# First six loads of gated values asked for one by one ahead of the down pass, with its first stores and code loads taken phase by phase

## The chip, the core and the metric

The kernel runs on one core of one Trainium2 chip. The metric is the device time of one execution in microseconds (us), as the median of several runs. Five engines work side by side, each in its own program order, and wait for one another by semaphores: TensorE (PE, matmuls, with a row PEld for weight loads), VectorE (DVE), ScalarE (ACT), GpSimd (POOL) and SyncE (SP). In this kernel POOL and SP mostly ask for DMA transfers, which the core's 16 DMA engines carry out.

## What is computed

Cross attention over a context, added to x, and then a feed-forward network whose three weight matrices are stored as 4-bit codes with one scale for each block of 64. The feed-forward part is what matters here:

```python
def dequant_nf4(q, absmax, shape):
    w = NF4_CODE[q.reshape(-1)]
    w = w.reshape(-1, BLOCK) * absmax[:, None]
    return w.reshape(shape)
Wg = dequant_nf4(gate_q, gate_absmax, (M, HD))
Wu = dequant_nf4(up_q, up_absmax, (M, HD))
Wd = dequant_nf4(down_q, down_absmax, (HD, M))
g = jnp.einsum('bsh,mh->bsm', x, Wg)
u = jnp.einsum('bsh,mh->bsm', x, Wu)
h = jax.nn.silu(g) * u
return jnp.einsum('bsm,hm->bsh', h, Wd)
```

HD is 1024, M is 3584, x has 8 x 256 rows. The codes come as 32-bit integers.

## The kernel before

**Stages.** Attention first, then the gate and up product, then the down product. Both products use a scheme of seven block products where a plain one has eight (Strassen's kind), and every operand is split into a high and a low float16 half (three matmuls for one product).

**Gate and up.** PE works through 392 slots (SLOT_COUNT) of 12 matmuls of 128 x 512. A slot reads a weight piece from one of the nine places of the tile wS. DVE and ACT combine and empty the PSUM banks, and form the gated values h (silu(g) times u). They are made for 14 pairs of chunks (CH_PAIRS), in seven forms and two sides for each pair. ACT copies a form's high half into one of four buffers, hst (line 2298), DVE writes its low half (line 2362), and POOL stores the buffer to the HBM tensor keep_h (line 2156). A buffer is free for the next copy when its store has landed.

**Down.** PE works through 98 steps (DOWN_STEPS, index m): seven groups (one for each form), of 14 steps each (one for each pair). Step m needs 512 KB of gated values, which POOL loads back from keep_h into one of six places, m % 6 (H_RING; line 2167): four in the tile `tail`, two in wS. It needs a decoded and transposed down weight too. A step is 24 matmuls, three in each of the eight banks. At the end of a group DVE empties the banks (lines 2404, 2410 and 2419), behind whatever DVE has in front of it, and PE's next group waits bank by bank. At step 0 each bank waits until DVE has taken the last gate and up results from it (line 2331); the third bank waits for all of them.

**Decode.** A unit is 128 x 512 codes. POOL or SP loads it into one of three places of the tile q (256 KB; line 285 for gate and up, line 288 for down). ACT makes ten squares (lines 343 and 347), DVE multiplies the factors (lines 376 and 363), both split the result into halves (lines 415, 422 and 431), and SP transposes it by DMA (line 302). There are 56 down units; their code loads begin during the last slots. The load of unit u waits until ACT has finished unit u − 3 and DVE has begun it. A planner (PLAN) lays down at which phase (slot or down step) each decode operation and each load stands in its engine's program order. Nothing else ties the engines' progress together but the semaphores.

**POOL's order.** In each slot k: the stores that are due (`stores_due`), the code loads that are due (`loads_due`) and, in the last four slots, one load of gated values (`load_h`). Then a wait until PE has ended all slots, and loads 4 and 5, whose places lie in wS. Step 0 of the down pass begins with the stores of three phases, then the code loads of three phases, then load 6. POOL carries this out strictly in order: an instruction that can't go on holds all that stand behind it.

Of the kernel before, what the change touches and what calls it, by code (L numbers as in the profile page):

```python
# [60 lines left out]
Q_RING, HALF_RING, SLOTS = 3, 5, 9  # L61
# [22 lines left out]
GATE_UP_PIECES = PIECES * STAGES  # L84
# [78 lines left out]
def piece_done(z):  # L163

    return slot_of(z // PIECES, z % PIECES, 1) + 1
# [1852 lines left out]
def feed_forward(nc, t, un, streams, st):  # L2018
# [6 lines left out]
    EVICT_BANK = {P2: X, P7: V, P3: Z, P4: Y}  # L2025
    EVICT_PLACE = {P2: (0, 0), P7: (1, 1), P3: (0, 1), P4: (1, 0)}
    HST_RING, H_RING = 4, len(t.h_in)
    EARLY_H = 4
    Q_AHEAD, ROWS_AT, Y_AT = 3, 1, 3
    BANKS = 8  # L2030
    FORM_BUF = {H_A11: 0, H_A22: 1, H_S1: 1, H_A12: 3, H_S3: 2, H_S2: 0, H_S4: 3}
    SUM_FORMS = (H_S1, H_S3, H_S2, H_S4)
    LAST_IN_BUF = (H_S2, H_S2, H_S3, H_S4)
# [26 lines left out]
    def down_freed(m):  # L2060

        group, c = m // CH_PAIRS, m % CH_PAIRS
        return (s_dn, BANKS * (group + 1)) if c == CH_PAIRS - 1 else (s_hd, (CH_PAIRS - 1) * group + c + 1)

# [81 lines left out]
    def gpsimd(pool):  # L2146
# [11 lines left out]
        def load_h(m):  # L2158
            if m < DOWN_STEPS:
                group, pair = m // CH_PAIRS, m % CH_PAIRS  # L2160
                form = GROUP_FORM[group]
                if m >= H_RING:
                    pool.wait_ge(*down_freed(m - H_RING))
                for side in range(2):
                    n = form_number(pair, form, side)
                    pool.wait_ge(s_hst[n % HST_RING], ring_count(n, HST_RING))
                nc.gpsimd.dma_start(t.h_in[m % H_RING].rearrange("p n a d -> p n (a d)"), t.hs[form, pair]).then_inc(s_hl[m % H_RING], 16)

        for k in range(SLOT_COUNT):
            stores_due(k)  # L2170
            loads_due(HIDDEN_PHASE + k)
            if k >= SLOT_COUNT - EARLY_H:
                load_h(k - SLOT_COUNT + EARLY_H)
        pool.wait_ge(s_mm, SLOT_COUNT)
        for m in range(EARLY_H, H_RING):
            load_h(m)
        for m in range(DOWN_STEPS):
            for ahead in range(Q_AHEAD) if m == 0 else (Q_AHEAD - 1,):
                if m + ahead < CH_PAIRS:
                    stores_due(SLOT_COUNT + m + ahead)  # L2180
            if m == 0:
                for ahead in range(Q_AHEAD):
                    loads_due(DOWN_PHASE + ahead)
            load_h(m + H_RING)
            loads_due(DOWN_PHASE + m + Q_AHEAD)
# [292 lines left out]
```

## Time and profile before

| what | value |
|---|---|
| median of 3 runs | 1928.77 us |
| lowest and highest run | 1926.29 and 1930.59 us |
| the profiled execution: its own time | 1936.15 us |
| the profiled execution: span in the trace | 1934.4 us |
| busy in the span: PE, PEld | 1899.4 us (98%), 961.7 us (50%) |
| busy in the span: DVE, ACT, POOL | 1624.6 us (84%), 1454.3 us (75%), 372.0 us (19%) |
| chain that ended last | PE 65%, ACT 15%, DVE 7%, issue 5%, DMA 2% |

Busy shares are means over stages with different limits. The chain that ended last is followed back from the last instruction: at each step to what released it. A timeline row gives the start, the duration, engine, line, operation, what is written and read, and in square brackets how long the engine had been idle before and on whom it waited. Idle time on an engine that isn't last costs nothing.

### The profile page before, as it was taken

How to read it: one execution, taken by the hardware profiler on the slowest of the kernel's cores; microseconds unless marked ns; L12 is line 12 of the kernel's file. 1: busy time of each engine (PE TensorE's matmuls, PEld its weight loads, DVE VectorE, ACT ScalarE, POOL GpSimd, SP SyncE). 2: the span in 40 equal slices, each digit the busy share in tenths (PEclk: the TensorE clock that was granted, in tenths of full speed). 3: DMA queues.
4: the chain of work that ended last, by engine and by line, in shares of the span. 5: the costliest groups of instructions: out<-in, count | busy, mean ns of one | idle time of the engine just before them, and what ended most of it. 6: DMA issues, size and time to landing. Idle time of an engine off the chain costs nothing.

```text
span 1934.4 us, 29450 instructions
## 1 busy us (share of the span) xinstructions
PE 1899.4 (98%) x9742; PEld 961.7 (50%) x9742; DVE 1624.6 (84%) x2673; ACT 1454.3 (75%) x2704; POOL 372.0 (19%) x570
## 2 busy tenths in 40 slices
PE   8999999999999999999999999999999999999999
PEld 3478888644444444444444444444443444444444
DVE  7968999878898898898898898898788898896963
ACT  2987676577988988988988988988979999900000
POOL 0013344321111121121121121121123222210010
PEclk9999999999999999999999999999999999999999
DMA  9347999954565464565464564555499999874462
GB/s 352 70 82 171 260 260 274 297 177 109 116 152 117 118 162 122 112 156 126 115 158 120 115 158 121 115 152 125 115 191 237 244 224 232 227 252 131 162 229 86
DMA packets 439257, 326.15 MB, mean 169 GB/s; under 512 B 373696, under 2 KB 373696, under 8 KB 437184
## 3 DMA queue, kind: packets, MB, share of 16 engines
q1 hardware_dynamic: 392848, 170.35, 40.8%
q0 software_dynamic: 44032, 153.65, 25.3%
q8 instruction: 77, 1.26, 0.3%
q10 hardware_dynamic: 2224, 0.27, 0.1%
q14 instruction: 76, 0.62, 0.1%
HBM read 154.31 MB, written 82.31 MB: 122 GB/s over the span
## 4 chain that ended last, share of the span: by engine, by line
PE 65%; ACT 15%; DVE 7%; issue 5%; DMA 2%; SPq 1%; POOL 0%; DVEq 0%; ACTq 0%; POOLq 0%
PE ps L2210 39%; PE ps L2252 19%; PE ps L1609 5%; ACT sq L347 5%; ACT sq L343 4%; ACT w L347 1%; PE ps L1577 1%; DVE w L363 1%; ACT w L343 1%; DVE tail L2362 1%; ACT halves L415 1%; PE ps L1644 1%; ACT tail L2283 1%; DMA T<-tail 1%; DVE halves L431 1%
## 5 line engine op out<-in xcount | busy, mean ns | idle before, releaser
L2210 PE MATMUL ps<-T,wS 128*128 128x512 f16 x4704 | 1017.6, 379 | 4.1 <-DVE ps L2317 2.5
L2210 PEld LDWEIGHTS ps<-T,wS 128*128 128x128 f16 x4704 | 459.8, 98 | 558.3 <-issue 4.8
L347 ACT ACTIVATE sq<-sq 128x512 f32<-128x512 f32 x898 | 515.1, 624 | 0.0
L363 DVE SCALAR_TENSOR_TENSOR w<-sq,w 128x512 f32<-128x512 f32 x590 | 416.5, 706 | 114.4 <-ACT sq L347 104.5
L343 ACT ACTIVATE sq<-q 128x512 f32<-128x512 int32 x598 | 361.9, 629 | 55.3 <-DVE w L363 47.7
L2252 PE MATMUL ps<-T,tail 128*128 128x512 f16 x1584 | 347.0, 380 | 10.0 <-DMA tail<-keep_h 3.6
L2252 PEld LDWEIGHTS ps<-T,tail 128*128 128x128 f16 x1584 | 155.0, 98 | 199.6 <-issue 13.7
L431 DVE SCALAR_TENSOR_TENSOR halves<-w,halves 128x512 f16<-128x512 f32 x240 | 163.8, 692 | 6.5 <-ACT halves L415 6.2
L2252 PE MATMUL ps<-T,wS 128*128 128x512 f16 x768 | 168.4, 379 | 0.2 <-DVE tail L2419 0.2
L2156 POOL DMA_DIRECT2D keep_h<-tail x196 | 106.3, 542 | 295.3 <-DVE tail L2362 294.7
L415 ACT CAST halves<-w 128x512 f16<-128x512 f32 x204 | 125.9, 619 | 41.2 <-DVE w L363 31.6
L2362 DVE SCALAR_TENSOR_TENSOR tail<-tail 128x512 f16<-128x512 f32 x196 | 133.7, 682 | 10.4 <-ACT tail L2298 10.2
L1609 PE MATMUL ps<-T 128*128 128x256 f16 x1152 | 128.7, 273 | 0.0
L2298 ACT CAST tail<-tail 128x512 f16<-128x512 f32 x196 | 119.6, 611 | 5.5 <-DVE tail L2331 5.5
L2252 PEld LDWEIGHTS ps<-T,wS 128*128 128x128 f16 x768 | 74.7, 98 | 91.4 <-DVE tail L2419 1.4
L1609 PEld LDWEIGHTS ps<-T 128*128 128x128 f16 x1152 | 112.6, 98 | 13.2 <-DMA T<-tail 0.3
L285 POOL DMA_DIRECT2D q<-in_L_ffn_up_q x52 | 28.0, 538 | 353.0 <-DVE w L363 256.9
L1508 POOL TENSOR_TENSOR T<-tail,T 128x256 f16<-128x256 f32 x64 | 58.9, 921 | 170.1 <-ACT T L1740 170.1
L288 POOL DMA_DIRECT2D q<-in_L_ffn_down_q x56 | 42.5, 759 | 229.5 <-DVE w L363 103.1
L2331 DVE SCALAR_TENSOR_TENSOR tail<-ps,up_out,tail 128x512 f32<-128x512 f32 x112 | 83.5, 746 | 2.1 <-PE ps L2210 1.1
L2283 ACT ACTIVATE tail<-ps,gate_out 128x512 f32<-128x512 f32 x112 | 75.8, 676 | 6.1 <-DVE ps L2321 3.7
L400 DVE TENSOR_TENSOR w<-w 128x512 f32<-128x512 f32 x112 | 76.8, 704 | 1.3
(229 smaller groups left out, 1870.5 us busy)
## 6 DMA issues: line engine op xcount, KB each, us to landing
keep_h<-tail POOLq DMA_DIRECT2D x196, 256.0 KB, 2.6
tail<-keep_h POOLq DMA_DIRECT2D x66, 512.0 KB, 4.9
wS<-keep_h POOLq DMA_DIRECT2D x32, 512.0 KB, 5.3
q<-in_L_ffn_down_q POOLq DMA_DIRECT2D x56, 256.0 KB, 4.4
T<-in_x SPq DMA_DIRECT2D x13, 1024.0 KB, 8.5
q<-in_L_ffn_up_q POOLq DMA_DIRECT2D x52, 256.0 KB, 3.0
q<-in_L_ffn_gate_q POOLq DMA_DIRECT2D x48, 256.0 KB, 3.5
keep_x<-T SPq DMA_DIRECT2D x38, 256.0 KB, 4.9
```

What stands on the lines that cost most here:

```text
L343: nc.scalar.activation(place, un.q[:, ring, :], ACT.Square, bias=b, scale=a).then_inc(un.s_act, 1)
L347: nc.scalar.activation(place, place, ACT.Square, bias=b, scale=a).then_inc(un.s_act, 1)
L363: nc.vector.scalar_tensor_tensor(out=out, in0=square_place(un, u, i - 1), scalar=FACTORS[i - 1][1], in1=un.w[:, buf, :], op0=ALU.add, op1= ...
L415: nc.scalar.copy(un.halves[:, z % HALF_RING, 0, :], source_of(un, t, z)).then_inc(un.s_whi, 1)
L431: nc.vector.scalar_tensor_tensor(out=un.halves[:, z % HALF_RING, 1, :], in0=source_of(un, t, z), scalar=1.0, in1=un.halves[:, z % HALF_RIN ...
L1609: last = nc.tensor.matmul(r_bank(o), t.A[:, a, k, o * P:(o + 1) * P], xT(b)[:, c, k, :], start=k == 0 and j == 0, stop=k == KT - 1 and j = ...
L2156: nc.gpsimd.dma_start(t.hs[form, pair, :, side, :], t.hst[:, n % HST_RING].rearrange("p a d -> p (a d)")).then_inc(s_hst[n % HST_RING], 16)
L2210: last = nc.tensor.matmul(ps[:, bank, :], un.wS[:, z % SLOTS, a, kt, :], t.Tp[side][product][:, :, b, kt, :], start=fresh and n == 0, stop ...
L2252: last = nc.tensor.matmul(ps[:, j, :], h[:, j // PAIRS, a, tok], quad(q, c)[:, b].rearrange("p k d -> p (k d)"), start=fresh and n == 0, s ...
L2283: nc.scalar.activation(t.act_buf[e], ps[:, EVICT_BANK[product] + side, :], ACT.Silu, scale=t.gate_out[:, 2 * pair + row:2 * pair + row + 1 ...
L2298: nc.scalar.copy(t.hst[:, n % HST_RING, 0, :], t.act_buf[2 * FORM_BUF[form] + side]).then_inc(s_hhi, 1)
L2362: nc.vector.scalar_tensor_tensor(out=t.hst[:, n % HST_RING, 1, :], in0=t.act_buf[2 * FORM_BUF[form] + side], scalar=1.0, in1=t.hst[:, n % ...
```

## The change

`EARLY_H` goes. A table H_AT names six slots, 26, 22, 18, 14, 8 and 4 before the end of the gate and up pass, and in each of them POOL now asks for one load of gated values, 0 to 5, behind that slot's stores and code loads. Loads 4 and 5 write into wS, whose pieces PE still reads then. They no longer wait for the end of all slots; each waits until PE has ended the last piece that was put into the places it overwrites (H_IN_W; pieces 190 and 192, ended by slots 382 and 386 in a count from one). At the start of the down pass the first three phases are taken one by one, stores and then code loads, where the stores of all three stood ahead of the code loads of all three.

```diff
-    EARLY_H = 4
+    H_AT = {SLOT_COUNT - at: m for m, at in enumerate((26, 22, 18, 14, 8, 4))}
...
+    H_IN_W = {m: max(z for z in range(GATE_UP_PIECES) if z % SLOTS in (2 * m - 8, 2 * m - 7)) for m in (4, 5)}
...
                 if m >= H_RING:
                     pool.wait_ge(*down_freed(m - H_RING))
+                elif m in H_IN_W:
+                    pool.wait_ge(s_mm, piece_done(H_IN_W[m]))
...
         for k in range(SLOT_COUNT):
             stores_due(k)
             loads_due(HIDDEN_PHASE + k)
-            if k >= SLOT_COUNT - EARLY_H:
-                load_h(k - SLOT_COUNT + EARLY_H)
-        pool.wait_ge(s_mm, SLOT_COUNT)
-        for m in range(EARLY_H, H_RING):
-            load_h(m)
+            if k in H_AT:
+                load_h(H_AT[k])
         for m in range(DOWN_STEPS):
             for ahead in range(Q_AHEAD) if m == 0 else (Q_AHEAD - 1,):
                 if m + ahead < CH_PAIRS:
                     stores_due(SLOT_COUNT + m + ahead)
-            if m == 0:
-                for ahead in range(Q_AHEAD):
+                if m == 0:
                     loads_due(DOWN_PHASE + ahead)
             load_h(m + H_RING)
             loads_due(DOWN_PHASE + m + Q_AHEAD)
```

Only POOL's order changes. On POOL, in the stretch from the last slots to the start of the down pass, stood before (keep_h<-tail is a store of gated values, tail<-keep_h and wS<-keep_h are the loads of them, q<-in_L0_ffn_down_q is a code load):

```order
L2156 DMA keep_h<-tail 128x1024 [waits s_hlo_f]
L288 DMA q<-in_L0_ffn_down_q 128x4x128 [waits s_fac,s_act]
L2167 DMA tail<-keep_h 128x2048 [waits s_hst1_f,s_hst0_f]
L2156 DMA keep_h<-tail 128x1024 [waits s_hlo_f]
L2167 DMA tail<-keep_h 128x2048 [waits s_hst3_f,s_hst2_f]
...
L2167 DMA wS<-keep_h 128x2048 [waits s_hst1_f,s_hst0_f,s_mm]
L2167 DMA wS<-keep_h 128x2048 [waits s_hst3_f,s_hst2_f]
L2156 DMA keep_h<-tail 128x1024 [waits s_hlo_f] x2
L288 DMA q<-in_L0_ffn_down_q 128x4x128 [waits s_fac,s_act] x2
L2167 DMA tail<-keep_h 128x2048 [waits s_hst1_f,s_hst0_f,s_hd_f]
```

and the same stretch, from load 4 on, stands now so:

```order
L288 DMA q<-in_L0_ffn_down_q 128x4x128 [waits s_fac,s_act] x3
L2170 DMA wS<-keep_h 128x2048 [waits s_hst1_f,s_hst0_f,s_mm]
L288 DMA q<-in_L0_ffn_down_q 128x4x128 [waits s_fac,s_act]
L2157 DMA keep_h<-tail 128x1024 [waits s_hlo_f]
L288 DMA q<-in_L0_ffn_down_q 128x4x128 [waits s_fac,s_act]
L2170 DMA wS<-keep_h 128x2048 [waits s_hst3_f,s_hst2_f,s_mm]
L2157 DMA keep_h<-tail 128x1024 [waits s_hlo_f] x4
L288 DMA q<-in_L0_ffn_down_q 128x4x128 [waits s_fac,s_act]
L2157 DMA keep_h<-tail 128x1024 [waits s_hlo_f]
L288 DMA q<-in_L0_ffn_down_q 128x4x128 [waits s_fac,s_act]
L2170 DMA tail<-keep_h 128x2048 [waits s_hst1_f,s_hst0_f,s_hd_f]
```

The six loads, which stood together with four stores, have moved out from between them. The first of the two code loads ahead of load 6 (unit 9) now stands behind four stores and ahead of one, where it stood behind all five.

Also on POOL, at the first down-code load, where the earliest of the six loads now stands; before, none stood here:

```order
L288 DMA q<-in_L0_ffn_down_q 128x4x128 [waits s_fac,s_act]
L2156 DMA keep_h<-tail 128x1024 [waits s_hlo_f] x5
L288 DMA q<-in_L0_ffn_down_q 128x4x128 [waits s_fac,s_act]
L2156 DMA keep_h<-tail 128x1024 [waits s_hlo_f] x4
L288 DMA q<-in_L0_ffn_down_q 128x4x128 [waits s_fac,s_act]
```

and now:

```order
L288 DMA q<-in_L0_ffn_down_q 128x4x128 [waits s_fac,s_act]
L2157 DMA keep_h<-tail 128x1024 [waits s_hlo_f] x2
L2170 DMA tail<-keep_h 128x2048 [waits s_hst1_f,s_hst0_f]
L2157 DMA keep_h<-tail 128x1024 [waits s_hlo_f] x3
L288 DMA q<-in_L0_ffn_down_q 128x4x128 [waits s_fac,s_act]
L2157 DMA keep_h<-tail 128x1024 [waits s_hlo_f]
L2170 DMA tail<-keep_h 128x2048 [waits s_hst3_f,s_hst2_f]
L2157 DMA keep_h<-tail 128x1024 [waits s_hlo_f] x3
```

Loads 0 and 1 stand among stores of gated values, three of which follow each of them directly.

## Rows read from the trace of the kernel before

**Rows 1.** Windows, middle of the down pass: columns in the first line, x counts instructions

```profile
core 0: us, PE busy (x) PEld busy (x) DVE busy (x) ACT busy (x) POOL busy (x), PEclk, DMA share, GB/s
1480.00:1600.00 120.00, 118.25 (x548) 52.93 (x547) 107.01 (x178) 120.00 (x232) 30.92 (x48) 1.00 1.00 236
```

**Rows 2.** Timeline of PE, down pass until the start of group 3

```profile
1412.28 1.46 PE L2252 MATMUL ps<-T,tail 128*128 128x512 f16 x6 [2.09 <-issue]
1414.60 19.60 PE L2252 MATMUL ps<-T,tail 128*128 128x512 f16 x90 [0.86 <-DVE tail L2331]
1434.04 10.52 PE L2252 MATMUL ps<-T,wS 128*128 128x512 f16 x48
1444.40 5.34 PE L2252 MATMUL ps<-T,tail 128*128 128x512 f16 x24
1450.45 5.34 PE L2252 MATMUL ps<-T,tail 128*128 128x512 f16 x24 [0.70 <-DMA tail<-keep_h]
1458.73 12.21 PE L2252 MATMUL ps<-T,tail 128*128 128x512 f16 x48 [2.94 <-DMA tail<-keep_h]
1470.77 10.52 PE L2252 MATMUL ps<-T,wS 128*128 128x512 f16 x48
...
1493.25 10.52 PE L2252 MATMUL ps<-T,tail 128*128 128x512 f16 x48 [1.60 <-DVE tail L2404]
...
1566.09 10.52 PE L2252 MATMUL ps<-T,wS 128*128 128x512 f16 x48 [0.16 <-DVE tail L2419]
...
1640.54 20.88 PE L2252 MATMUL ps<-T,tail 128*128 128x512 f16 x96 [1.78 <-DVE tail L2410]
```

**Rows 3.** Windows, the stretch behind PE's longest wait (columns as in rows 1)

```profile
1460.00:1464.00 4.00, 4.00 (x14) 1.52 (x13) 3.29 (x6) 4.00 (x9) 1.56 (x3) 0.66 1.14 173
```

**Rows 4.** Timeline of ACT around its wait for a code load

```profile
1410.53 2.19 ACT L347 ACTIVATE sq<-sq 128x512 f32<-128x512 f32 x4
...
1428.90 1.15 ACT L347 ACTIVATE w<-w 128x512 f32<-128x512 f32 x2
...
1437.03 1.15 ACT L343 ACTIVATE sq<-q 128x512 f32<-128x512 int32 x2 [6.99 <-DMA q<-in_L_ffn_down_q]
```

**Rows 5.** Timeline of POOL: code loads (L288), a store (L2156), loads (L2167)

```profile
1394.92 0.76 POOL L288 DMA_DIRECT2D q<-in_L_ffn_down_q  x1 [5.44 <-DVE w L363]
...
1413.59 1.13 POOL L2167 DMA_DIRECT2D wS<-keep_h  x2
...
1421.55 0.55 POOL L2156 DMA_DIRECT2D keep_h<-tail  x1 [5.45 <-DVE tail L2362]
1431.08 0.77 POOL L288 DMA_DIRECT2D q<-in_L_ffn_down_q  x1 [8.98 <-DVE w L363]
1437.38 0.76 POOL L288 DMA_DIRECT2D q<-in_L_ffn_down_q  x1 [5.53 <-issue]
...
1442.40 0.55 POOL L2167 DMA_DIRECT2D tail<-keep_h  x1
...
1447.54 0.53 POOL L2167 DMA_DIRECT2D tail<-keep_h  x1 [0.58 <-issue]
```

**Rows 6.** Issue to landing (last number, us): DMAs of 1413.6, 1421.6, 1431.1, 1442.4, 1447.5, 1408.2

```profile
wS<-keep_h POOLq DMA_DIRECT2D x2, 512.0 KB, 17.5
...
keep_h<-tail POOLq DMA_DIRECT2D x1, 256.0 KB, 13.7
...
q<-in_L_ffn_down_q POOLq DMA_DIRECT2D x1, 256.0 KB, 5.9
...
tail<-keep_h POOLq DMA_DIRECT2D x1, 512.0 KB, 7.9
...
tail<-keep_h POOLq DMA_DIRECT2D x1, 512.0 KB, 11.1
...
keep_h<-tail POOLq DMA_DIRECT2D x1, 256.0 KB, 4.7
```

**Rows 7.** Timeline of POOL and ACT: a store, and the copy that reuses its buffer

```profile
1345.18 0.54 POOL L2156 DMA_DIRECT2D keep_h<-tail  x1 [1.85 <-DVE tail L2362]
...
1352.40 0.60 ACT L2298 CAST tail<-tail 128x512 f16<-128x512 f32 x1
```

## The prediction

> **What bounds the kernel now.** I read the busy time of the engines by stretches first, then TensorE (PE) in order of time around the start of the down pass, then the GpSimd queue (POOL), the landing times of its DMAs, and ScalarE (ACT) and VectorE (DVE) beside them. In the down pass PE is nearly full, but it isn't alone: from 1480 to 1600 us PE works 118.25 of 120 us, and ACT, which decodes the down weights, works 120.00 of 120 [rows 1]. So there are two chains that run side by side, PE's steps and the ACT/DVE decode, and they meet where DVE has to empty the PSUM banks between groups.
>
> PE's steps: two steps (48 matmuls) take 1444.40 − 1434.04 = 10.36 us, so a step is 5.18 us and a matmul 0.216 us [rows 2]. What PE loses after 1410 stands in its idle notes [rows 2]: 2.09 us before step 0, 0.86 us at its third bank, which waits for DVE's last eviction; 0.70 us and 2.94 us at steps 7 and 8, for loads of gated values; 1.60, 0.16 and 1.78 us at 1493.25, 1566.09 and 1640.54, the starts of groups 1, 2 and 3, where DVE's eviction is late. Steps 6 to 9 take 1470.77 − 1444.40 = 26.37 us instead of 20.72: a loss of 5.65 us, of which 3.64 is shown as idle time. Much of the rest is the clock: from 1460 to 1464 us the granted clock is 0.66, between its two levels of 2.4 and 1.2 GHz, just after the idle 2.94 us [rows 3].
>
> The decode: ACT ends a unit's squares at 1428.90 + 1.15 = 1430.05 and then idles 6.99 us, until 1437.03, for a code load [rows 4]. That load, unit 9 (the tenth down-code request), is asked for by POOL at 1431.08 and takes 5.9 us to land [rows 5, 6]. Its counters ask only that ACT has finished unit 6 (1410.53 + 2.19 = 1412.72 [rows 4]) and DVE has begun it. POOL's last instruction before it, a store, began at 1421.55 and ended at 1422.10, so POOL stood 9 us with its named conditions fulfilled [rows 5]. What does end then is the landing of the two loads of gated values issued at 1413.59 and right after: 17.5 us, thus about 1431.1 to 1431.7 [rows 5, 6]. The next code load starts at 1437.38, 0.35 us after the one before landed, with no releaser that the profile can name [rows 5]. I read this as a limit on what POOL's DMA queue can hold: six loads of 512 KB put in within 7 us block the next code load, and a code load is blocked until an earlier one is consumed. Six of them are 3 MB, and stores lie among them.
>
> **Part 1: the six loads leave the crowd.** They are the same instructions, each asked for once. POOL time is unchanged; it has idle time before nearly each of them. The first now stands just ahead of the store at 1345.18 [rows 7], the fifth just behind the code load at 1394.92 [rows 5], the sixth two code loads later, where the first stood. The values are of pairs 0 to 5 and were stored long before. Loads 4 and 5 wait for PE's slots 382 and 386, which end 10 and 6 slots ahead of PE's change to the down pass at 1410.2: at 2.59 us a slot, 1384.3 and 1394.6. POOL reaches load 4 only after 1394.92 + 0.76 [rows 5], and load 5 later still. No new wait ends last, cost 0; were POOL early, a code load would stand behind it.
>
> Step 0 now finds its load: the 2.09 us go. But the third bank still waits for DVE's eviction, until 1414.60 [rows 2], and nothing here makes that eviction earlier. So these 2.09 us come back as waiting, 2.95 in place of 0.86 us plus the six matmuls, and the gain is 0.
>
> **Part 2: code loads and stores, phase by phase.** POOL now asks for code load 9 before the store that began at 1421.55, thus between 1413, when unit 6 is finished, and 1422.10. Either is enough: with the 5.9 us of [rows 6] it lands between 1419 and 1428, before 1430.05. So on its own this interleaving is worth 0, and the work that hides it is unit 8 on ACT; it gives code load 10 some room. Code load 10 needs unit 7 finished on ACT. ACT does 232 operations in 120 us [rows 1], 0.517 us each, and a unit has ten: 5.2 us. So unit 7 ends about 1424.9. Asked for then, code load 10 may take 10.3 us before ACT wants it at 1435.2. Load 6 follows at about 1425.6 instead of 1438, loads 7 and 8 at about 1435 and 1440 instead of 1442.40 and 1447.54 [rows 5]. With their old 7.9 and 11.1 us [rows 6] they land at 1443 and 1451; steps 7 and 8 begin without gaps at 1449.6 and 1454.8. The 0.70 and 2.94 us go, and the clock's part with them.
>
> **The sum.** PE alone could win a lot: without a gap from 1414.60, group 3 would start 42 steps less six matmuls later, 217.56 − 1.30 = 216.26, at 1630.86 instead of 1640.54: 9.68 us. But there DVE's eviction ends last, and it stands behind the decode. That chain has no other idle time worth the name between 1437.03 and 1640; so it moves by what it idles now, 6.99 us. Group 1, whose start waits for DVE, goes from 1493.25 to 1486.3 where PE alone gives 1485.8; group 2 at 1559.1 (PE 1558.8), group 3 at 1633.5. After group 3 PE runs through and nothing gives the gain back. The sum is 6.99 us, with 0 and 9.68 us as the ends.
>
> At step 0 there is one unknown, the clock. Now the idle time there is in two pieces; afterwards it is one piece of some 3.1 us, a little over the 2.94 us that was followed by the lower clock [rows 2, 3]. If that happens, PE loses 5.65 − 3.64 = 2.0 us, at most. Group 1 then starts at 1487.8 and group 2 at 1560.3, later than DVE allows; at group 3 DVE ends last again, and the loss is absorbed. From below it costs 0; I take 0 for the end time.
>
> A page of the Trainium skill bears on the landing times. The row says 17.5 us for a load of 512 KB in the crowd [rows 6]. The Trainium skill's "DMA: Bandwidth & Descriptors", section "Anatomy of one DMA — SWDGE (gpsimd) path", fits a DMA's time as 2.0 us plus its bytes over 436 GB/s, 3.2 us by an estimate for 512 KB, and some 12 us for the six and four stores together. By that rule the crowd would be gone when POOL is through its stores at 1422.10, no code load would be held, and the time would be that of the first rival below; the row contradicts it.
>
> **Rivals.**
>
> *The hold stays* (no gain). If POOL stands at 1422 for another reason than landings, the decode chain moves by 0. PE still wins its 5.65 us at steps 6 to 9 and then waits for DVE at 1493.25 as long as now. Time unchanged, 1928.8. For it: the profile names DVE as releaser at 1431.08. Against it: that counter was satisfied long before, and two starts agree with landings to within half a microsecond.
>
> *The load moves but lands slowly* (half the gain). Transposes keep the DMA engines busy in this stretch: a store of 256 KB issued at 1421.55 took 13.7 us [rows 6]. At that price code load 9 lands at 1429.8, just in time, but code load 10 at 1424.9 + 13.7 = 1438.6 instead of 1435.2. The chain gives back 3.4 us and 3.6 remain: 1925.2. Against it: without 3 MB ahead of it that store would hardly take this long.
>
> *The crowd moves to the stores* (slower). From 1343 on, each of the first loads stands ahead of stores, which free the four buffers into which ACT copies gated values. The store of 1345.18 must have landed when ACT copies at 1352.40 [rows 7]: 7.2 us of room. A store behind a load took 4.7 us at 1408 [rows 6]; as slow as in the crowd, 13.7, it would hold ACT 6.5 us at each of two places, loads 0 and 1. That is 13.0 less the 7.0 won: 6.0 us slower, 1934.8. It decides when a store takes over about 7 us. The rule beside it: the Trainium skill's "Trainium Kernel Development and Optimization", section "Key Constraints", says that DMAs issued from the three queues share the same 16 engines and interleave, so an earlier load is not free.
>
> *PE alone decides* (more gain). If DVE weren't the last at groups 1 to 3, up to 9.68 us: 1919.1.
>
> **How the numbers follow.** The profiled execution took 1936.15 us with a span of 1934.4, the runs have a median of 1928.77. The difference lies outside the stretches used, so the 7.0 us are taken from the median: 1921.8; a profiled execution should give about 1929.2. Chances: forecast 0.68, half the gain 0.14, no gain 0.10, slower 0.05, more gain 0.03. The range reaches from the PE bound, 1919.0, over the half gain to 1926.5, with about 1 us for the spread of runs (1926.3 to 1930.6). About 0.2%, 3.9 us, is what a measurement of this kernel can tell from no change: 1924.9 is the line. Nearly all of the forecast's and the larger gain's chance lies below it, and little of the half gain's: faster 0.72, same 0.23, slower 0.05.
>
> **What would show it.** Code load 9 asked for at 1415 to 1423, with no wait of ACT for down codes near 1430. Loads 4 and 5 landing in under 9 us. No PE wait for gated values after step 0, and the start of group 3 about 7 us earlier against the change to the down pass. Step 0's first two banks start at once, and the third still waits for DVE. I am wrong if ACT still idles there, if ACT's copies wait for stores between 1345 and 1365, or if DVE's eviction delays take back what PE won.

## The result, and the profile after

| what | before | after |
|---|---|---|
| median of 17 runs each, side by side | 1927.04 us | 1931.62 us |
| lowest and highest run | 1926.14 and 1933.53 us | 1928.55 and 1938.69 us |
| the profiled execution: its own time | 1936.15 us | 1929.53 us |
| the profiled execution: span | 1934.4 us | 1927.7 us |

The kernel became slightly slower: the ratio after/before is 1.0019, with a 95% interval from 1.0010 to 1.0028, or 3.7 us (1.9 to 5.4); the two medians lie 4.6 us apart. 1921.8 us was forecast, with a range up to 1926.5. The two traced executions say the opposite: after's is 6.6 us the shorter. So the first thing to see is that before's traced execution lies 9.1 us above the median of its own kernel, and after's 2.1 us below.

Timeline of PE in the kernel after, around the start of the down pass and at the start of group 3 (columns as in [rows 2]; the down pass stands at L2251 now):

```profile
1409.62 1.46 PE L2251 MATMUL ps<-T,tail 128*128 128x512 f16 x6
1415.08 21.29 PE L2251 MATMUL ps<-T,tail 128*128 128x512 f16 x90 [3.99 <-DVE tail L2330]
1436.20 10.52 PE L2251 MATMUL ps<-T,wS 128*128 128x512 f16 x48
1446.56 20.88 PE L2251 MATMUL ps<-T,tail 128*128 128x512 f16 x96
1467.28 7.93 PE L2251 MATMUL ps<-T,wS 128*128 128x512 f16 x36
...
1633.91 20.88 PE L2251 MATMUL ps<-T,tail 128*128 128x512 f16 x96 [0.71 <-DVE tail L2409]
```

Against [rows 2], the 2.09 us ahead of step 0 and the 0.70 and 2.94 us of steps 7 and 8 are gone, and groups 1 and 2 start without a gap. The wait at the third bank has grown from 0.86 to 3.99 us. From that bank to the start of group 3 it is 1633.91 − 1415.08 = 218.83 us, before 1640.54 − 1414.60 = 225.94: 7.11 us won, where 6.99 was the forecast.

Timeline of POOL after. The third down-code load with load 2 behind it, then the stretch of [rows 5]:

```profile
1360.50 0.77 POOL L288 DMA_DIRECT2D q<-in_L_ffn_down_q  x1 [3.15 <-DVE w L363]
1361.26 0.54 POOL L2157 DMA_DIRECT2D keep_h<-tail  x1
1361.79 0.54 POOL L2170 DMA_DIRECT2D tail<-keep_h  x1
...
1415.93 0.54 POOL L2157 DMA_DIRECT2D keep_h<-tail  x1 [3.69 <-DVE tail L2361]
1418.17 0.77 POOL L288 DMA_DIRECT2D q<-in_L_ffn_down_q  x1 [1.70 <-DVE w L363]
1422.02 0.54 POOL L2157 DMA_DIRECT2D keep_h<-tail  x1 [3.08 <-DVE tail L2361]
1425.28 0.76 POOL L288 DMA_DIRECT2D q<-in_L_ffn_down_q  x1 [2.72 <-ACT sq L347]
1426.03 0.55 POOL L2170 DMA_DIRECT2D tail<-keep_h  x1
```

Code load 9 is asked for at 1418.17 and code load 10 at 1425.28, where [rows 5] has 1431.08 and 1437.38. Nothing holds POOL there, and ACT no longer waits for a code load in this stretch. But ACT has a wait of another kind, 50 us earlier. Waits of 1355 to 1376 us (engine, line, waited for: total, times, longest), then the timelines of ACT and of SP's transposes, all of after:

```profile
ACT halves L415 <- DMA wS<-halves: 2.9, 1, 2.9
```
```profile
1364.31 1.64 ACT L415 CAST halves<-w 128x512 f16<-128x512 f32 x3
1368.82 0.62 ACT L415 CAST halves<-w 128x512 f16<-128x512 f32 x1 [2.86 <-DMA wS<-halves]
```
```profile
1361.07 11.47 SPq L302 DMA_TRANSPOSE wS<-halves  x6
```

The same places in the kernel before:

```profile
1366.79 2.19 ACT L415 CAST halves<-w 128x512 f16<-128x512 f32 x4
```
```profile
1363.55 9.97 SPq L302 DMA_TRANSPOSE wS<-halves  x6
```

The tile `halves` has five places. ACT fills one with a high half (line 415), DVE adds the low half (line 431), SP transposes it into the weights (line 302), and the place is free when that transpose has landed. Before, ACT made four such casts without a break; now the fourth waits 2.86 us. Six transposes in a row took 9.97 us before and 11.47 us now, and load 2 was issued at 1361.79, 0.7 us after the first of them. It took 6.8 us to land, thus until 1368.6, and ACT went on at 1368.82:

```profile
tail<-keep_h POOLq DMA_DIRECT2D x1, 512.0 KB, 6.8
```

**The account of the two traces.** From the third down-code load to the third bank of step 0 it is 1415.08 − 1360.50 = 54.58 us after. Before, that code load stands at 1362.91, and it is 1414.60 − 1362.91 = 51.69: 2.89 us lost, the size of ACT's new wait. Behind it 7.1 us are won. (PE loses part of it as well: 0.93 and 0.80 us of waiting in after's last slots, where before has none.) And already at the third down-code load before's trace was 2.41 us behind after's (at the first down-code load 1339.98 against 1337.50, 2.48): work ahead of everything that the change touches. It arises where POOL loads x back from HBM: the row of seven such loads starts at 373.09 in before and 371.39 in after, the next one at 382.52 and 379.96, and from there on the distance stays near 2.5 us. 7.1 + 2.4 − 2.9 = 6.6 us, the difference of the traced executions.

That can also be set against the medians, and this is argument, not measurement: 1936.15 less the 7.0 us of the hold and the 2.4 us lag is 1926.8, before's median of 1927.04. So a typical execution of before in this comparison seems to have had no hold to lose, and to it the change only adds ACT's wait: 1926.8 + 2.9 = 1929.7, after's traced 1929.53. After's median is 2 us above that. No second execution of before was traced; what the other traces say to it stands in the part on why the prediction was wrong.

### The profile page after: what moved, and what is told of

Same layout as the page of the kernel before. It is cut to its first block, busy times and chain, and to the rows that moved or that the text cites. A ratio compares the mean times of both kernels' runs of the same rounds, so it can differ in the third digit from the quotient of the medians.

```text
span 1927.7 us, 29450 instructions
## 1 busy us (share of the span) xinstructions
PE 1897.1 (98%) x9742; PEld 961.8 (50%) x9742; DVE 1623.6 (84%) x2673; ACT 1454.5 (75%) x2704; POOL 372.4 (19%) x570
## 4 chain that ended last, share of the span: by engine, by line
PE 63%; ACT 18%; DVE 6%; issue 5%; DMA 2%; POOL 0%; SPq 0%; DVEq 0%; ACTq 0%; POOLq 0%
PE ps L2209 39%; PE ps L2251 15%; PE ps L1609 6%; ACT sq L347 6%; ACT sq L343 5%; ACT w L347 2%; ACT w L343 2%; DVE w L363 1%; PE ps L1577 1%; PE ps L1644 1%; DVE tail L2361 1%; ACT halves L415 1%; ACT tail L2282 1%; DMA T<-tail 1%; ACT tail L2297 1%
## 5 line engine op out<-in xcount | busy, mean ns | idle before, releaser
L2251 PE MATMUL ps<-T,tail 128*128 128x512 f16 x1584 | 346.5, 380 | 4.7 <-DVE tail L2330 4.0
L2251 PEld LDWEIGHTS ps<-T,tail 128*128 128x128 f16 x1584 | 155.2, 98 | 193.4 <-DVE tail L2330 4.5
L2251 PE MATMUL ps<-T,wS 128*128 128x512 f16 x768 | 168.4, 379 | 0.0
L2251 PEld LDWEIGHTS ps<-T,wS 128*128 128x128 f16 x768 | 75.1, 98 | 90.6
L288 POOL DMA_DIRECT2D q<-in_L_ffn_down_q x56 | 42.6, 760 | 229.7 <-DVE w L363 116.8
```

The costliest lines, as they stand in the source:

```text
L2251: last = nc.tensor.matmul(ps[:, j, :], h[:, j // PAIRS, a, tok], quad(q, c)[:, b].rearrange("p k d -> p (k d)"), start=fresh and n == 0, s ...
```

## The experiments

What had to be told apart: (A) an ordinary execution of before has no hold, and the cost is load 2 beside the transposes; (H) the hold belongs to the kernel, and the loss is elsewhere. In all of them the 334 DMA transposes are replaced by plain DMA copies of as many bytes between the same tiles, so the operands aren't turned and the values differ, while all other instructions, waits and loops stay. No variant with the transposes themselves was run, so what follows for them rests on how alike the two behave, and where they don't is said. The common edit, "the base" from here on:

```diff
+PIECE = 128
...
+def plain(sp, dst, src, size=PIECE):
...
+    n = 1024 // size
+    rows = bass.AP(tensor=src.tensor, offset=src.offset, ap=[list(src.ap[0]), [size - 2, n], [1, size]])
+    return sp.dma_start(dst, rows)
...
-    sp.dma_start(dst, un.halves[:, z % HALF_RING, :, :].rearrange("p a c -> p (a c)"), transpose=True).then_inc(
+    dst = dst.rearrange("p k m -> p (k m)").rearrange("p (x m) -> p x m", m=64)
+    plain(sp, dst, un.halves[:, z % HALF_RING, :, :].rearrange("p a c -> p (a c)"), 64).then_inc(
```

Differences of medians below come with a 95% interval from resampling the runs. Only kernels that ran side by side are compared: the names with the same first letter belong together.

### How like a transpose is a copy?

c1_copy256 copies in packets of 256 bytes everywhere, q1_base128 copies the weights in packets of 128 bytes; q2_after128 is q1_base128 with the whole change. Each ran once.

> The kernel before, in which each of the 334 DMA transposes is a plain copy of as many pieces of 256 bytes between the same places (the weights and keys then aren't transposed). It is the base for the tests that follow. If a plain copy costs the DMA engines about what a transpose costs, the time is within 0.5% of before, six copies in a row near 1362 us take 9 to 12 us as the transposes do, and their landing stays near 6 us in the down pass. Theory A (the hold near 1430 us belonged to one execution): ACT idles under 1 us for a code load at the start of the down pass. Theory B (it is in every execution): 6 to 8 us.

> The kernel before with plain copies in place of all DMA transposes, the weight pieces' now in packets of 128 bytes, twice as many as a transpose has, to cost the DMA engines about what transposes cost (37.6% of their time from 1380 to 1480 us; the copy in 256-byte packets took 17.7%). Expected: 30 to 40%, six copies in a row near 1362 us take 9 to 12 us. Theory A: the hold of POOL near 1430 us comes when the crowd of six loads meets such busy engines, for some executions only: ACT idles 0 to 7 us. Theory B (in every execution): 6 to 8 us.

> The changed kernel with the same copies. Theory A (load 2 is asked for beside six turned pieces in a row and delays them; ACT and DVE then wait for a free half buffer): ACT waits 1.5 to 4 us for a copy wS<-halves between 1355 and 1375 us, and PE's step 0 waits 3 to 5 us for DVE's last eviction. Rival (the wait in the changed kernel's trace belonged to that execution): no such wait.

Copies and transposes aren't alike, and not in one direction. Shares of the time of the 16 DMA engines that the transposes take, and the copies in their place:

| stretch | before | after | c1_copy256 | q1_base128 |
|---|---|---|---|---|
| 1380 to 1480 us (around the crowd) | 37.6% | 28.9% | 17.7% | 25.1% |
| 1355 to 1375 us (six in a row, where load 2 comes) | 41.3% | 40.8% | 34.0% | 61.5% |

Around the crowd the 128-byte copies take less than the 30 to 40% expected and less than the transposes (whose share depends on the crowd too: it is smaller in after, which has none); in the six in a row they take more. The six take 9.97 us in before, 7.98 in c1_copy256 and 10.71 in q1_base128 (9 to 12 expected). Neither kernel with copies has a hold: code load 9 is asked for 0.81 us after the last store has begun in c1_copy256 and 0.77 us in q1_base128. But this says little about before. c1_copy256 took 1925.17 us where before beside it took 1928.29, and q1_base128 1927.44 where before took 1935.24; in the five comparisons that follow, before's median lies 5.7 to 8.0 us above that of the unchanged kernel with copies. What the transposes cost there may be the hold, and the copies can't show it.

q2_after128 took 1928.03 us. ACT's wait for a half buffer is 2.19 us in it and 0.91 us in the base, and the third bank waits 3.99 us, as theory A has it. With one run each the times decide nothing here.

### Which part of the change costs the time?

Same base. t2_after128 is the whole change; t3_later128 moves loads 2 and 3 away from the transposes; t4_load2_128 moves load 2 alone:

```diff
-    H_AT = {SLOT_COUNT - at: m for m, at in enumerate((26, 22, 18, 14, 8, 4))}
+    H_AT = {SLOT_COUNT - at: m for m, at in enumerate((26, 22, 13, 11, 8, 4))}
```
```diff
-            if k >= SLOT_COUNT - EARLY_H:
+            if k == SLOT_COUNT - 18:
+                load_h(2)
+            if k >= SLOT_COUNT - EARLY_H and k != SLOT_COUNT - EARLY_H + 2:
```

> The kernel before with plain copies in packets of 128 bytes in place of the weight transposes, timed. Base for the next three. Both theories: about 1925 to 1928 us. In it ACT waits 0.9 us for a half buffer near 1365 us.

> The changed kernel with the same copies, timed. Theory A (only the ACT/DVE chain matters, and it is delayed by what load 2 adds to ACT's wait for a half buffer, 2.19 instead of 0.91 us): 1.3 us over the base, between 0.5 and 2.5. Rival (the change itself costs the 3.7 us that the ratio 1.0019 gives, by some other way, such as PE's idle time of 3.99 us at step 0): 3 to 5 us over the base.

> As the one before, but loads 2 and 3 asked for 13 and 11 slots ahead of the end, behind the six copies in a row. Theory A: ACT's wait is back at 0.9 us, the time within 0.7 us of the base. Rival: as the one before, 3 to 5 us over the base.

> The base with load 2 alone asked for 18 slots ahead of the end; the other five stay in the crowd. Theory A: all of the loss without the rest of the change, 1.3 us over the base (0.5 to 2.5), ACT's wait 2.2 us. Rival: within 0.7 us of the base, since PE's idle time at step 0 and the order of the rest are as before.

| kernel | median (runs) | against the base | ACT's wait for a half buffer |
|---|---|---|---|
| t1_base128 | 1927.40 (7) | | 1.08 us |
| t2_after128 | 1928.74 (9) | +1.3 (0.6 to 2.5) | 2.39 us |
| t3_later128 | 1927.97 (7) | +0.6 (−1.0 to 1.9) | 0.94 us |
| t4_load2_128 | 1929.45 (12) | +2.1 (0.8 to 3.2) | 1.92 us |

Timeline of ACT at that cast (line 426 in these kernels), in the order of the table:

```profile
1367.76 0.62 ACT L426 CAST halves<-w 128x512 f16<-128x512 f32 x1 [1.08 <-DMA wS<-halves]
```
```profile
1367.63 0.62 ACT L426 CAST halves<-w 128x512 f16<-128x512 f32 x1 [2.39 <-DMA wS<-halves]
```
```profile
1365.19 0.62 ACT L426 CAST halves<-w 128x512 f16<-128x512 f32 x1 [0.94 <-DMA wS<-halves]
```
```profile
1373.38 0.62 ACT L426 CAST halves<-w 128x512 f16<-128x512 f32 x1 [1.92 <-DMA wS<-halves]
```

Load 2 alone, moved to 18 slots before the end, costs time, and with the loads away from there the wait is back at the base's. The wait of the whole change grew by 1.31 us and its time by 1.3; from the whole change to t3_later128 the time falls by 0.8 us (−2.7 to 0.5), which alone isn't clear of the noise. t4's excess is larger than its wait (0.84 us more than the base's), within its interval.

The traces say more than the medians here, if each is cut in three: up to the first down-code load (nothing of the change lies ahead of it), from there to the third bank of step 0, and from there to the end of the span. w0 to w2, x1 and x2 are kernels of the sections below, w0_base128 is the base again:

| trace | its time | start to first code load | to the third bank | ACT's wait for a half buffer | third bank to end |
|---|---|---|---|---|---|
| before | 1936.15 | 1339.98 | 74.62 | none | 519.8 |
| after | 1929.53 | 1337.50 | 77.58 | 2.86 | 512.6 |
| w0_base128 | 1926.62 | 1336.38 | 75.75 | 1.04 | 512.7 |
| t2_after128 | 1928.48 | 1336.79 | 77.09 | 2.39 | 512.7 |
| t3_later128 | 1926.67 | 1335.79 | 75.65 | 0.94 | 513.4 |
| t4_load2_128 | 1934.10 | 1343.01 | 76.62 | 1.92 | 512.7 |
| w2_two128 | 1931.99 | 1339.80 | 77.57 | 2.87 | 512.8 |
| w1_ring768 | 1940.90 | 1344.56 | 75.14 | 0.46 | 519.4 |
| x1_ring768 | 1941.38 | 1345.46 | 75.28 | 0.60 | 518.9 |
| x2_after_ring768 | 1937.49 | 1344.68 | 75.25 | 0.57 | 515.8 |

The middle part is before's 74.62 us plus ACT's wait, within 0.1 us in every row, with transposes as with copies. So what load 2 adds to that wait reaches the third bank in full. The last part is 512.6 to 513.4 us in every row in which POOL isn't held. And the first part differs by 7.2 us between the four rows w0_base128 to t4_load2_128 alone, which are the same program up to there: t4_load2_128's traced execution is 7.5 us longer than w0_base128's without any hold, 6.6 of it ahead of the first code load (w0_base128 above, t4_load2_128 below):

```profile
1336.38 0.78 POOL L288 DMA_DIRECT2D q<-in_L_ffn_down_q  x1 [3.02 <-DVE w L374]
```
```profile
1343.01 0.78 POOL L288 DMA_DIRECT2D q<-in_L_ffn_down_q  x1 [3.02 <-DVE w L374]
```

That distance, 6.6 us, is there in full at the first code load of the gate and up pass behind the loads of x (427.94 against 434.53) and stays.

The Trainium skill's "Trainium Kernel Development and Optimization", section "Key Constraints", says that DMAs of the three queues share the 16 engines; t4_load2_128 shows what this means for a load put beside SP's work.

t3_later128 shows another thing. Timeline of its PE at the third bank of step 0:

```profile
1411.44 19.60 PE L2262 MATMUL ps<-T,tail 128*128 128x512 f16 x90 [4.00 <-DVE tail L2341]
```

PE idles 4.00 us here, as in after, at the time of the base within the noise. So this idle time costs nothing that could be measured at the end: DVE decides. That was the forecast's reading of step 0. The clock doesn't fall behind this wait (it is granted in full from 1412 to 1420 us, and the 90 matmuls take the usual 19.60 us). In t2_after128 it falls to 0.50 from 1414 to 1418 us and they take 22.27 us, but from the third bank to the end it is 512.72 us there and 512.67 in w0_base128, whose 90 matmuls take 19.60: the lower clock is absorbed as well.

### Do slow copies make the hold?

v1_base_slow copies five of the first down weights (pieces 5 to 9) in 64-byte packets, to keep the DMA engines busy in the crowd's time:

```diff
-    plain(sp, dst, un.halves[:, z % HALF_RING, :, :].rearrange("p a c -> p (a c)"), 64).then_inc(
+    size = 32 if 5 <= z - GATE_UP_PIECES <= 9 else 64
...
+    plain(sp, dst, un.halves[:, z % HALF_RING, :, :].rearrange("p a c -> p (a c)"), size).then_inc(
```

> The base with copies, in which the five weight pieces turned around the start of the down pass (down units 5 to 9) go in packets of 64 bytes, four times a transpose's number, so that the DMA engines are busy just when the crowd of six loads meets them. Theory H (POOL's queue holds only so many requests; when the crowd drains slowly, the next code load can't be put in): loads 4 and 5 take over 12 us to land, POOL stands before code load 9 for 3 us or more with its counters fulfilled, ACT idles for it, and the time is 3 to 8 us over the base's 1927.4. Rival: POOL asks for code load 9 within 1 us of its last store as in the base, and only landings are late; ACT idles under 2 us.

1927.48 us (10 runs), and POOL asks for code load 9 at 1420.52, right behind its store. Theory H expected a hold and none came. But the crowd wasn't slow either: loads 4 and 5 land in 8.0 us where over 12 were expected (9.2 in w0_base128). So this run didn't make the condition, and says nothing against theory H:

```profile
1420.52 0.77 POOL L288 DMA_DIRECT2D q<-in_L_ffn_down_q  x1 [0.21 <-ACT sq L359]
```

### Does the room in POOL's queue make the hold?

The program reserves room for the descriptors of POOL's DMAs with one number, 1024 in all kernels so far:

```diff
-    nc = bacc.Bacc("TRN2", target_bir_lowering=False, num_devices=1, dynamic_dma_scratch_size=1024)
+    nc = bacc.Bacc("TRN2", target_bir_lowering=False, num_devices=1, dynamic_dma_scratch_size=768)
```

w1_ring768 and x1_ring768 are the base with 768, x3_ring1536 with 1536, x2_after_ring768 the whole change with 768. Beside w1, w3_interleave128 has only part 2 (stores and code loads phase by phase), and w2_two128 is the whole change with loads 2 and 3 both at 18 slots before the end.

> The base with copies in 128-byte packets once more, as the measure for the three beside it. 1927.4 us as before, within 1 us; ACT waits 0.9 to 1.1 us for a half buffer near 1366 us.

> The base with the room for the descriptors of POOL's DMA queue cut from 1024 to 768 bytes (a code load has 512 rows of 512 bytes, a store or a load of gated values 128 rows). Theory H (POOL is held when its queue has no room): POOL stands, with fulfilled counters, between the code load near 1404 us and the second or third request behind it until that code load has landed, some 4 us after it was asked for, and again near the end of the crowd; with ACT's code loads late by that the time is 0 to 4 us over the base. Rival (the queue's room plays no part): POOL's starts differ from the base's by less than 0.5 us.

> The changed kernel with copies, loads 2 and 3 both asked for 18 slots ahead of the end, beside the six copies in a row. Theory A (each load there adds 1.3 us to ACT's wait for a half buffer, and the end moves with it): ACT waits 3.2 to 3.8 us, 2.3 to 3.3 us over the base. Rival (the end doesn't follow that wait): within 1.5 us of the base.

> The base with copies and only the second part of the change, stores and code loads at the start of the down pass taken phase by phase. Theory A: code load 9 has time to spare either way, within 0.5 us of the base. Rival (the interleaving helps the decode by an earlier code load): 1 to 3 us below the base.

> The base with copies in 128-byte packets, as the measure for the three beside it: 1926 to 1928 us.

> The base with a POOL DMA queue of 768 bytes again, as the measure for the next: 16 to 20 us over the base; POOL asks for code load 9 only when the crowd has landed, and ACT idles 1 to 3 us for it.

> The changed kernel with copies and the same short queue. Theory H (where the crowd holds POOL, the change wins what the hold costs): POOL asks for code load 9 before 1420 us, counted as in the base, ACT doesn't idle for it, and the time is 2 to 7 us under the short-queue base (it gives back 1.3 us at load 2). Rival (the hold costs nothing that the change could win): 0 to 3 us over the short-queue base.

> The base with copies and a queue of 1536 bytes. Theory H: with copies, 1024 bytes hold POOL nowhere that counts, so the time is within 1 us of the base. Rival (the queue's room costs time all along): 2 us or more below the base.

| kernel | median (runs) | against | difference |
|---|---|---|---|
| w0_base128 | 1926.57 (12) | | |
| w1_ring768 | 1944.93 (4) | w0 | +18.4 (14.3 to 19.6) |
| w2_two128 | 1928.60 (12) | w0 | +2.0 (0.9 to 3.1) |
| w3_interleave128 | 1926.98 (12) | w0 | +0.4 (−0.6 to 1.3) |
| x0_base128 | 1927.61 (9) | | |
| x1_ring768 | 1943.40 (9) | x0 | +15.8 (13.7 to 19.0) |
| x2_after_ring768 | 1938.08 (10) | x1 | −5.3 (−8.3 to −2.9) |
| x3_ring1536 | 1925.78 (8) | x0 | −1.8 (−3.3 to −0.4) |

**The hold can be made.** Timeline of POOL in w1_ring768 (loads of gated values at L2178, stores at L2167), and the landing of the store of 1424.68:

```profile
1418.96 0.54 POOL L2178 DMA_DIRECT2D tail<-keep_h  x1 [0.17 <-issue]
1421.49 0.53 POOL L2178 DMA_DIRECT2D wS<-keep_h  x1 [1.99 <-issue]
1422.29 0.53 POOL L2178 DMA_DIRECT2D wS<-keep_h  x1 [0.27 <-issue]
1424.68 0.55 POOL L2167 DMA_DIRECT2D keep_h<-tail  x1 [1.86 <-issue]
1426.65 0.55 POOL L2167 DMA_DIRECT2D keep_h<-tail  x1 [1.42 <-DVE tail L2373]
1432.11 0.77 POOL L288 DMA_DIRECT2D q<-in_L_ffn_down_q  x1 [4.91 <-ACT w L354]
1436.94 0.77 POOL L288 DMA_DIRECT2D q<-in_L_ffn_down_q  x1 [4.06 <-issue]
```
```profile
keep_h<-tail POOLq DMA_DIRECT2D x1, 256.0 KB, 7.1
```

Nothing but the room has changed, and POOL now stops inside the crowd with no releaser, then stands 4.91 us ahead of code load 9 and goes on 0.3 us after the store of 1424.68 has landed (1431.8). For POOL it is the picture of [rows 5], down to the second stop ahead of code load 10 and a releaser named that the profile can't have meant. For ACT it isn't: behind code load 9 it idles 1.48 us where [rows 4] has 6.99, and in x1_ring768 it doesn't idle for a code load before 1478 us (w1_ring768 above, x1_ring768 below), where 1 to 3 us for code load 9 were expected:

```profile
1436.63 1.15 ACT L354 ACTIVATE sq<-q 128x512 f32<-128x512 int32 x2 [1.48 <-DMA q<-in_L_ffn_down_q]
```
```profile
1478.59 1.15 ACT L354 ACTIVATE w<-q 128x512 f32<-128x512 int32 x2 [1.33 <-DMA q<-in_L_ffn_down_q]
```

The same base with the usual room, w0_base128, has this in place of the stop ahead of code load 9:

```profile
1420.31 0.77 POOL L288 DMA_DIRECT2D q<-in_L_ffn_down_q  x1 [0.69 <-ACT sq L358]
```

x1_ring768 repeats POOL's stop, with code load 9 at 1431.67. In this kernel, where POOL is held, the change takes time off, 5.3 us, within the 2 to 7 expected: code loads 9 and 10 start at 1423.10 and 1430.06 in x2_after_ring768. Between the two traces it is 3.9 us, of which 3.1 lie behind the third bank (518.9 and 515.8). So POOL's queue does hold it when it has no room, and the change then wins in the down pass. That it wins through code load 9, as the forecast has it, is not shown: ACT's waits for code loads sum to 4.7 us in x1_ring768 and 2.8 in x2_after_ring768, all of them from 1477 us on.

**The size was missed.** 0 to 4 us were expected of the smaller room, and it costs 16 to 18. The hold at the down pass is a part only: of the 14.3 us between the traces of w1_ring768 and w0_base128, 8.2 lie ahead of the first down-code load and 6.7 behind the third bank. POOL's longest waits without a releaser in x1_ring768, at line 1325 (POOL's loads of x back from HBM, between 370 and 400 us at the start of the gate and up pass) and at the stores, then the longest in x0_base128 and in x3_ring1536:

```profile
POOL T L1325 <- issue: 16.6, 6, 5.3
POOL keep_h L2167 <- issue: 16.6, 10, 2.5
```
```profile
POOL T L1325 <- issue: 12.1, 5, 4.5
```
```profile
POOL tail L2178 <- issue: 0.4, 1, 0.4
```

With 1536 the 12.1 us at line 1325 are gone altogether, so they were a hold by the same queue (the traced before stands there for 12.4 us), and the kernel is 1.8 us faster, more than the "within 1" expected and less than the rival's 2.

**The interleaving alone** (w3) can't be told from 0, as forecast. **Two loads beside the transposes** (w2) lengthen ACT's wait to 2.87 us (3.2 to 3.8 expected) where w0 has 1.04. The excess, 2.0 us, is 1.8 us of more wait within its error, and a little under the 2.3 to 3.3 expected. One load there made the wait grow by 1.31 us (t2_after128 against t1_base128), so the second adds 0.5 us and not another 1.3:

```profile
1371.13 0.62 ACT L426 CAST halves<-w 128x512 f16<-128x512 f32 x1 [2.87 <-DMA wS<-halves]
```

### Is there something to win in moving the loads well?

With the room at 1536 and loads 2 and 3 at the places of t3, against the unmoved loads:

> The base with copies and a queue of 1536 bytes once more: 1925 to 1926.5 us, POOL nowhere held before the attention's T tiles (12 us in the base).

> The changed kernel with copies, loads 2 and 3 at 13 and 11 slots ahead of the end and a queue of 1536 bytes. Theory A (the end follows the ACT/DVE chain, and nothing of the early loads is on it once load 2 is behind the six copies): within 0.7 us of the long-queue base. Rival (early loads still win something at step 0): 1 to 3 us below it.

y0_ring1536 took 1926.01 us and y1_later_ring1536 1925.43 (12 runs each): −0.6 (−1.4 to 0.7). ACT's wait for a half buffer is 0.8 us in both. Away from the six copies in a row the move costs nothing that could be measured, and it brings nothing either.

## Why the prediction was wrong

**The time of the traced execution, the step that failed.** "The difference lies outside the stretches used, so the 7.0 us are taken from the median." The 7.4 us between the traced time and the median shown were about the size of the stall, and that should have been the warning. An execution 7 us slower than its median, with a 7 us stall whose two starts hang on how fast DMAs happen to land, is one in which the stall may well be the reason. What the runs showed in its place: before's median in the comparison was 1927.04 us, and the change took nothing off it. The parts of the table say how far this can be trusted. With the hold, before would need at least 1335.8 us (the shortest first part of any trace with the usual room, of a kernel with copies; before's was 1340.0) + 74.6 + 519.8 us of span, and 1.8 us between span and time: 1932.0 us by this estimate. Of before's 17 executions in the comparison 16 lie below, so they hardly had it. This is worked out, not traced. It holds for that comparison only: of the 114 executions of before beside the other experiments 77 lie above 1932.0.

Taken from the trace, 1936.15 − 6.99 = 1929.2, the sum seems to hold for the traced execution ("should give about 1929.2": it gave 1929.53). That is luck in part: 2.9 us of loss that nobody forecast and 2.4 us by which after's execution was ahead from the start cancel out.

**Part 1 at cost 0, the second step that failed.** The loads were tried against the stores and their four buffers, PE's slots and POOL's idle time, but not against SP's transposes and the five places of `halves`. Load 2 stands beside six transposes in a row. ACT, and the decode chain with it, pays 2.86 us in the trace, and that reaches the third bank in full; of the measured 3.7 us this is the larger part. In the copies it is 1.3 us for the whole change and 2.1 for load 2 alone. Lighter copies don't explain the smaller cost, since in this stretch the 128-byte copies take more of the DMA engines' time than the transposes; the base with copies has a wait of 0.9 to 1.1 us there from the start, and before has none. What the other 1 us or so of the 3.7 is, stays open.

**The hold as a limit of POOL's queue: borne out in kind.** With less room POOL stops at the same two code loads and goes on when earlier DMAs land, and with more room its stops at the loads of x are gone. That the stop of the traced before itself would go with more room was not run, and with the smaller room ACT loses at most 1.5 us for code load 9, not 7.

**The sum of 6.99 us for a trace that has the hold: right**, 7.11 from the third bank to group 3. Groups 1 and 2 start without a gap of PE, at group 3 DVE ends last again, with 0.71 us of waiting, and the gain of PE alone (9.68 us) is not reached.

**Step 0: right in kind.** Its first two banks start at once and the wait goes over to the third, 3.99 us where about 3.1 was worked out; DVE comes later than before by the wait that ACT got. PE itself comes to step 0 later too, by 1.8 us counted from the third down-code load (1409.62 − 1360.50 = 49.12 us, before 1412.28 − 2.09 − 1362.91 = 47.28), so its wait at the third bank grows by 1.0 us and not by 2.9. The clock does dip there. Windows of after (columns as in [rows 1]):

```profile
1412.00:1416.00 4.00, 0.92 (x3) 0.37 (x4) 4.00 (x7) 2.84 (x6) 0.31 (x2) 0.92 0.60 186
1416.00:1420.00 4.00, 4.00 (x13) 1.51 (x12) 3.97 (x8) 2.19 (x4) 1.24 (x2) 0.66 0.38 107
```

A granted clock of 0.66, between the two levels, follows the idle 3.99 us, as it followed 2.94 us in [rows 3]; behind the 4.00 us of t3_later128 none follows. The 90 matmuls take 21.29 us instead of 19.60 in [rows 2], 1.7 us against the bound of 2.0 (2.7 in t2_after128), and the equal last parts of t2_after128 and w0_base128 show that it is absorbed, as was forecast.

**Part 2 at 0: right** (w3), and code load 9 came at 1418.17, within the 1415 to 1423 given. Loads 4 and 5 landed in 3.9 and 4.1 us, under the 9 given.

**The rivals.** By its time, 1928.8, "The hold stays" lies 2.8 us from after's median; as a change it gave 0 where 3.7 us were lost, and "The crowd moves to the stores" gave 6.0. Neither has the reason: in the trace the hold goes, but in most executions of the comparison it was hardly there. The Trainium skill's fit ("DMA: Bandwidth & Descriptors", section "Anatomy of one DMA — SWDGE (gpsimd) path"), which was set beside it, makes an estimated 3.2 us for 512 KB. The moved loads took from 3.9 to 6.8 us in after; the fit is nearer to these than to the 17.5 us of [rows 6]. "The crowd moves to the stores" had the kind of thing right, an early load that holds up ACT through a buffer, and the wrong victim: the first stores behind loads 0 and 1 took 3.9 and 5.9 us, under the 7 us from which it decides, and ACT waits for no store there. It was given 0.05, and slower 0.05 as a whole; a load moved into a stretch whose other DMA users hadn't been listed deserved far more.

**What stays open.** Why the crowd drained so slowly in the traced before: from 1424 to 1428 us the DMA share is above 1 while 84 GB/s are moved:

```profile
1424.00:1428.00 4.00, 4.00 (x21) 1.77 (x19) 3.93 (x7) 4.00 (x9) 0.00 (x0) 1.00 1.30 84
```

Of that share 82.6 points are the transposes', for 0.11 MB, and the three transposes issued between 1411 and 1431 us took 20.0, 16.2 and 11.5 us to land, where the four of after, without the crowd, took 3.5 to 5.5. In w0_base128 the copies of that stretch took 4.5 to 11.9 us, and loads 4 and 5 took 9.2 instead of 17.5. So the copies don't meet the crowd as the transposes do, and the runs with copies can't say how often before has the hold. Beside the experiments before's median was from 1932.2 to 1935.5 us, with runs from 1926.8 to 1945.7, a far wider spread than the base with copies had (1925.8 to 1930.4). The hold may be in many of those, and then the change might win in them; a late first part as in t4_load2_128 may be it as well. After, which has no crowd, has runs up to 1938.69 too. After ran only beside the 1927.04, and before was traced only once.

## What to carry to other kernels

Set a traced execution's own time beside the median before a stall is priced: if the excess is about the size of the stall, the stall may belong to that execution, and its gain may not be there in the median. Cut the trace in parts ahead of, within and behind what the change touches, and compare the parts, not the totals: here the part ahead of it differed by up to 7.2 us between traces of kernels that were the same up to there. A DMA that is moved early has to be held, at its new place, against every other user of the DMA engines there that has a ring of buffers behind it, transposes above all, not only against its own queue and buffers. Where GpSimd stands without a named releaser amid its own DMAs, try the room of its DMA queue first: here, with copies in place of the transposes, 768 instead of 1024 cost 16 to 18 us, and 1536 won 1.8.

## What was not expected of the hardware

- Room in POOL's DMA queue weighs on stages far from the crowd: 12.1 us of POOL's standing near 380 us, among its loads of x, were gone with 1536, and the whole kernel lost 15.8 to 18.4 us with 768 (all with copies).
- One load of 512 KB beside six transposes stretched these from 9.97 to 11.47 us and stopped ACT for 2.86 us, while the load itself took 6.8 us where others took 3.9.
- Transposes beside the crowd of six loads took 11.5 to 20.0 us to land in before, and 3.5 to 5.5 us in the same stretch of after, which has no crowd.
- Neither transposes nor copies are the heavier ones in every stretch: from 1380 to 1480 us the transposes of before took 37.6% of the DMA engines' time (28.9% in after) and the 128-byte copies 25.1%; from 1355 to 1375 us it was 41.3% against 61.5%.
